# Quantised tiles from row scales in memory in the place of a transpose, in a two-layer kernel on one core

## The chip, the cores and the metric

The kernel runs on one core of a Trainium2 chip. The core has five engines with a queue each: TensorE (PE, matrix products into PSUM), VectorE (DVE), ScalarE (ACT), GpSimd (POOL) and SyncE (SP), which here issues nearly all transfers between memory and SBUF. The metric is the device time of one execution in microseconds. Before the change it is 2084.08 us, the median of three runs (2083.98 to 2085.03).

## What is computed

Two layers over x of 2 x 4096 tokens with 512 channels. In each layer x is normalised, goes through a mixing part and a feed-forward part, and both are added to x. The change touches the feed-forward part of the first layer, a product with x and weights in a 6-bit block format:

```
def _mx_quantize(t, eps=1e-30):
    rows, K = t.shape
    blocks = t.reshape(rows, K // BLOCK_SIZE, BLOCK_SIZE)          # BLOCK_SIZE = 32 channels
    scales = jnp.maximum(jnp.max(jnp.abs(blocks), axis=-1) / FP6_E2M3_MAX, eps)
    q = _nearest_on_grid(blocks / scales[..., None], _GRID)
    return (q, scales)
...
    xq, xs = _mx_quantize(x2)
    wq, ws = _mx_quantize(w2)
    xd = (xq * xs[..., None]).reshape(x2.shape)
    wd = (wq * ws[..., None]).reshape(w2.shape)
    out = xd @ wd.T + bias
...
    x = L0_attn_x
    xn = _layernorm(x, axis=-1)
    x = x + _L0_attn_ref(xn, ...) + _L0_ffn_ref(xn, L0_ffn_weight, L0_ffn_bias)
    xn = _layernorm(x, axis=-1)
    x = x + _L1_attn_ref(xn, ...) + _L1_ffn_ref(xn, ...)
```

`_L0_attn_ref` is two projections, a depthwise convolution, a state-space scan and an output projection; `_L1_attn_ref` is linear attention, whose sums over keys and values are gathered while the first layer's sums are made.

## The kernel before

All work is written out by hand, engine by engine; each engine runs its own list in order, and semaphores join them. Nothing is scheduled by a planner. There are four stages.

**Projection** (`phase_project`, the first 350 us or so). 16 groups of 512 tokens. Per group SP loads x by tokens (for its statistics), x by channels (`x_turned`, 1 MB) and the mean and the root as rows, broadcast over the partitions (`load_rows`). DVE makes the statistics (`statistics`) and normalises x by channels in place (`normalise`, L380, L383); ACT and DVE split it into a high and a low part, since a product in full precision is made of three products; PE projects twice. For the rows, SP stores mean and root to memory (`store_rows`, L244), element by element. The first two groups are normalised by tokens and turned on PE.

**Scan** (`phase_scan`). 64 octets of channels. At its end ACT, DVE, POOL and PE already prepare the first tiles of the next stage.

**Mixing** (`phase_mix`, about 530 to 1300 us). 64 tiles of 128 tokens; the loop variable N of every engine's list stands for the tile whose sums are made. For tile N:
- PE adds two products into the bank of the sums: the scanned part (`scanned`, operand u) and the quantised part (`forward`, operand `qt`). Then it turns the normalised sums of tile N - 1 (`turn_sums`, operand `xn`) and the quantised tile N + 1 (`turn_q`, operand `xq`), both by `turn_in` at L1452, four transposes of 128 x 128. Then `outer` (L1496) of tile N - 3 and `keys` of tile N - 2. It is 48 products of 512 columns and 8 transposes per tile.
- DVE: `low_keys` of N - 3 (L1339); seven steps that quantise tile N + 2 with tokens on the partitions (`prepare_step`, L1311 to L1327: the largest value of each block, scale, inverse, multiply, exponent, rounding number, add it); in even tiles `gate` (L1290), which multiplies u for the next two tiles; `sums` of N (L1348 to L1359), which takes the bank and makes the statistics; `low_n` (L1334); `low_q` of N + 1 (L1296), the low half of the turned quantised tile, out of the bank `BB`; `low_nat` (L1364).
- POOL: `add_keys` of N - 3 (L1113); the root and the shift of the normalisation of tile N (L1117, L1120); in odd tiles `low_u` for the next two (L1105); `finish_quantising` of N + 2: subtract the rounding number (L1084), multiply by the scales (L1086).
- ACT: `keys` (L1197, L1200), `set_keys` (L1189), in odd tiles `high_u` (L1155), `take_turned` (L1206, L1210), `set_sums` (L1179), `high_q` (L1159), `normalise_sums` (L1219, L1224), and `normalise_input` of tile N + 3 (L1167).
- SP: in odd tiles the load of u (y and v, 512 KB each); the store of the sums; the load of x for four tiles on; every second tile a store of the turned sums.

`xq` has three buffers, `qt` two. **Second layer** (`phase_second_layer`): 16 groups; its weights take over buffers of the mixing stage, and its first weights are split on ACT and DVE from tile 50 on.

## Time and profile before

| | us |
|---|---|
| median of three runs | 2084.08 |
| lowest and highest | 2083.98, 2085.03 |
| the profiled execution, its own time | 2084.98 |
| its span | 2083.2 |

| engine | busy us | share |
|---|---|---|
| PE | 2065.6 | 99% |
| DVE | 1521.2 | 73% |
| ACT | 1095.3 | 53% |
| POOL | 839.5 | 40% |

The page gives busy time, the span in 40 slices, the DMA queues, the chain that ended last and the costliest groups of instructions. The engines wait for one another through semaphores, so a busy share doesn't tell how much an engine can be lengthened; the timeline of one stretch does. Two matmuls in a row overlap in the records: a product of 512 columns is recorded with 0.39 us, and the next one starts 0.23 us after it. So on PE starts are to be compared, not durations. TensorE's clock is at its upper level nearly throughout (mean 0.998).

### The profile page before, as it was taken

To read this page: it belongs to the slowest core of one execution; us is meant where nothing else is said; L and a number is where in the kernel's file an instruction comes from. 1 tells how busy PE (TensorE), PEld (TensorE's weight loads), DVE (VectorE), ACT (ScalarE), POOL (GpSimd) and SP (SyncE) were. 2 spreads that over 40 slices of the span, in tenths; PEclk is the share of its full clock that TensorE was granted. 3 is DMA by queue.
4 is the path that set the end of the run, shared out by engine and by line. 5 is a ranking of instruction groups with operands and counts; after the bars stand their busy time and mean duration, and the time that the engine had idled before them with its cause. 6 is when DMAs were issued, how large, how long until landed. Compare 5 with 4: busy or idle time off the path is not lost.

```text
span 2083.2 us, 27336 instructions
## 1 busy us (share of the span) xinstructions
PE 2065.6 (99%) x9263; PEld 1647.1 (79%) x9263; DVE 1521.2 (73%) x2943; ACT 1095.3 (53%) x1842; POOL 839.5 (40%) x842
## 2 busy tenths in 40 slices
PE   9999999999999999999999999999999999999998
PEld 7787888444688888888888888788888888888887
DVE  5898785666687777777777875677777676667776
ACT  4555556323455555555555555754455555555453
POOL 1001110355545444454445453144444444444444
PEclk9999999999999999999999999999999999999999
DMA  5997883886533333333333333422222222222211
GB/s 186 235 222 221 202 219 116 280 255 211 178 115 118 102 118 105 116 118 102 122 107 117 103 128 104 152 71 72 71 71 71 92 91 81 92 71 72 71 41 41
DMA packets 193637, 263.46 MB, mean 126 GB/s; under 512 B 34265, under 2 KB 124633, under 8 KB 190938
## 3 DMA queue, kind: packets, MB, share of 16 engines
q1 hardware_dynamic: 180376, 238.18, 37.7%
q10 hardware_dynamic: 13122, 23.53, 3.0%
q8 instruction: 74, 1.21, 0.2%
q14 instruction: 65, 0.53, 0.1%
HBM read 160.88 MB, written 100.79 MB: 126 GB/s over the span
## 4 chain that ended last, share of the span: by engine, by line
PE 89%; DVE 5%; ACT 2%; issue 2%; POOL 1%; DMA 1%; SPq 0%; POOLq 0%; ACTq 0%
PE bank L102 23%; PE bank L104 23%; PE bank L103 22%; PE bank L1496 7%; PE bank L2052 3%; PE bank L885 3%; PE bank L906 3%; PE bank L903 3%; PE bank L1452 2%; PE bank L629 1%; DVE e_w_lo L1879 0%; DVE d_x L1348 0%; DVE d_xq L1319 0%; DVE d_stats L1350 0%; PE bank L1510 0%
## 5 line engine op out<-in xcount | busy, mean ns | idle before, releaser
L102 PE MATMUL bank<-e_ring,e_w_hi 128*128 128x512 f32 x512 | 200.8, 392 | 0.0
L103 PE MATMUL bank<-e_ring,e_w_hi 128*128 128x512 f32 x512 | 199.3, 389 | 0.0
L104 PE MATMUL bank<-e_ring,e_w_lo 128*128 128x512 f32 x512 | 199.3, 389 | 0.0
L1496 PE MATMUL bank<-d_kh,d_nat 128*128 128x512 f32 x768 | 191.1, 398 | 0.0
L1772 POOL TENSOR_TENSOR e_x<-e_x,e_beta 128x512 f32<-128x512 f32 x64 | 91.3, 1446 | 220.7 <-ACT e_y L1815 220.7
L1117 POOL TENSOR_TENSOR rstd<-d_var_eps,neg_half 128x1 f32<-128x1 f32 x64 | 35.6, 556 | 340.5 <-DVE d_var_eps L1359 340.5
L1826 ACT ACTIVATE e_kr<-bank 128x512 f32<-128x512 f32 x64 | 38.0, 593 | 247.6 <-PE bank L104 247.6
L1496 PEld LDWEIGHTS bank<-d_kh,d_nat 128*128 128x128 f32 x768 | 139.7, 188 | 26.9
L1897 DVE TENSOR_TENSOR e_ring<-e_mixed,e_ring 128x512 fp32r<-128x512 f32 x128 | 93.5, 731 | 88.1 <-ACT e_ring L1790 88.0
L1754 POOL TENSOR_TENSOR e_x<-e_x,e_ff 128x512 f32<-128x512 f32 x64 | 83.3, 1302 | 175.6 <-DVE e_ff L1963 175.6
L1364 DVE TENSOR_TENSOR d_nat<-d_xn,d_nat 128x512 fp32r<-128x512 f32 x64 | 85.9, 1344 | 77.7 <-ACT d_nat L1224 77.7
L1888 DVE SCALAR_TENSOR_TENSOR e_mixed<-e_xt,cols,e_prev 128x512 f32<-128x512 f32 x128 | 104.0, 813 | 41.3 <-ACT e_prev L1801 40.7
L1206 ACT ACTIVATE d_xt<-bank 128x512 f32<-128x512 f32 x64 | 38.2, 597 | 166.9 <-PE bank L1452 166.9
L757 DVE TENSOR_TENSOR_SCAN c_state<-decay,bank 128x255 f32<-128x255 f32 x128 | 80.5, 670 | 52.8 <-PE bank L885 52.6
L308 POOL TENSOR_TENSOR b_rstd<-b_var_eps,neg_half 128x4 f32<-128x4 f32 x16 | 16.2, 1010 | 255.0 <-DVE b_var_eps L364 255.0
L102 PEld LDWEIGHTS bank<-e_ring,e_w_hi 128*128 128x128 f32 x512 | 96.1, 188 | 20.4 <-issue 0.9
L1790 ACT ACTIVATE e_ring<-e_mixed 128x512 fp32r<-128x512 f32 x128 | 80.7, 632 | 59.8 <-DVE e_mixed L1888 57.5
L1758 POOL TENSOR_TENSOR e_y<-e_y,e_att 128x512 f32<-128x512 f32 x64 | 107.0, 1671 | 12.8 <-DVE e_att L1982 12.8
L104 PEld LDWEIGHTS bank<-e_ring,e_w_lo 128*128 128x128 f32 x512 | 96.1, 188 | 20.0
L103 PEld LDWEIGHTS bank<-e_ring,e_w_hi 128*128 128x128 f32 x512 | 96.1, 188 | 19.3
L102 PE MATMUL bank<-e_w_hi,e_keys 128*128 128x512 f32 x256 | 103.7, 405 | 0.1
L102 PE MATMUL bank<-b_xt,b_v 128*128 128x512 f32 x256 | 100.8, 394 | 2.7 <-ACT b_vt L557 2.7
(222 smaller groups left out, 6298.0 us busy)
## 6 DMA issues: line engine op xcount, KB each, us to landing
scr_v<-b_vt SPq DMA_DIRECT2D x64, 256.0 KB, 3.5
scr_z<-b_zt SPq DMA_DIRECT2D x64, 256.0 KB, 5.6
c_z<-scr_z SPq DMA_DIRECT2D x64, 256.0 KB, 4.3
scr_y<-c_y ACTq DMA_DIRECT2D x64, 256.0 KB, 3.9
d_x<-in_L_attn_x SPq DMA_DIRECT2D x64, 256.0 KB, 3.8
d_v<-scr_v SPq DMA_DIRECT2D x32, 512.0 KB, 5.1
scr_x<-d_x SPq DMA_DIRECT2D x64, 256.0 KB, 2.3
scr_xnt<-d_xt SPq DMA_DIRECT2D x32, 512.0 KB, 4.1
```

The costliest lines, as they stand in the source:

```text
L102: eng.matmul(out, lhs[hi], rhs[hi], start=first, stop=False, skip_group_check=onto)
L103: eng.matmul(out, lhs[hi], rhs[lo], start=False, stop=False, skip_group_check=onto)
L104: return eng.matmul(out, lhs[lo], rhs[hi], start=False, stop=last, skip_group_check=onto)
L757: nc.vector.tensor_tensor_scan(state[o % 2][:, b, 1:], rate, SB[o % 2][:, b * NCB:(b + 1) * NCB - 1], 0.0, ALU.mult, ALU.add).then_inc(sta ...
L1364: nc.vector.tensor_tensor(nat[q][:, 1, :], xn[N % 2][:, :], nat[q][:, 0, :].bitcast(F32), ALU.subtract).then_inc(nat_lo, 1)
L1496: mm = pe.matmul(BG[c][:, :], s[:, i, cols], r[:, j, :], start=M % NTB == 0 and i == j, stop=M % NTB == NTB - 1 and i == 1, skip_group_che ...
L1754: nc.gpsimd.tensor_tensor(x2[h][:, t, :], x2[h][:, t, :], ff[t % 2][:, :], ALU.add).then_inc(base_done, 1)
L1758: nc.gpsimd.tensor_tensor(y[t][:, :], y[t][:, :], att[t % 2][:, :], ALU.add).then_inc(sum_done, 1)
L1772: nc.gpsimd.tensor_tensor(x2[h][:, t, :], x2[h][:, t, :], beta[:, :], ALU.add).then_inc(shifted, 1)
L1790: nc.scalar.activation(ring[slot][:, 0, kt, :], src, ACT.Copy).then_inc(hi_done, 1)
L1888: nc.vector.scalar_tensor_tensor(mixed[kt % 2][:, :], current(g % 2, kt), mu[:, kt:kt + 1], prev[kt % 2][:, :], ALU.mult, ALU.add).then_in ...
L1897: nc.vector.tensor_tensor(ring[slot][:, 1, kt, :], src, ring[slot][:, 0, kt, :].bitcast(F32), ALU.subtract).then_inc(lo_done, 1)
```

## The change

From tile 8 on (`BY_ROWS`), x is quantised with channels on the partitions, so that the quantised tile needs no turn before `forward` uses it.

In the mixing stage, for a tile N from 8 to 63:
- SP loads the tile by tokens (`load_tokens`), ACT normalises it (`normalise_tokens`, in the place of `normalise_input`), DVE makes scales and inverses per token and block (`scale_tile`, four steps, the last a transpose of 128 x 32 in blocks of 32 x 32), SP stores them (`store_scales`, 16 KB).
- SP then loads the inverses as a row per block, broadcast over the 32 channels of the block (`load_channels`, 256 KB), and with them the tile by channels out of a new array in which the projection stage has stored normalised x (256 KB); later the scales in the same way (`load_scales`, 256 KB).
- DVE multiplies by the inverse rows, and makes the three rounding steps as before (`row_step`); POOL subtracts, and multiplies by the scale rows. ACT's `high_q` and DVE's `low_q` read the finished tile from SBUF, not from the bank.
- PE leaves `turn_q` out.

In the projection stage SP stores the normalised x of groups 2 to 15 (1 MB each), and the statistics are turned on DVE (`turn_statistics`, two transposes of 128 x 32 per group) and stored in rows of 128 bytes by eight transfers, where two stored single elements. `load_channels` of that stage waits for the low parts alone, behind the store.

What else is in the diff serves room and semaphores: the first buffer `gt` lies where weights of the second layer will be, so their load (at tile 40) and split (at tile 50) wait for PE's use of it; four row buffers lie where the second `gt` will be; several counters are merged into one, with the same waits; the first loads of the scan wait for the stores of normalised x; the second layer's first load waits for `low_q` of the last tile in the place of its turn.

The core of the diff:

```diff
+        def store_normalised(g):
+            if g > TURNED_GROUPS:
+                sp.wait_ge(xn_stored, 16 * (g - TURNED_GROUPS))
+            sp.wait_ge(xn_done, 2 * KT * g)
+            sp.dma_start(scr["xn"][g], xc[g % 2][:, :, :]).then_inc(xn_stored, 16)
...
         def store_rows(g):
-            sp.wait_ge(stat, 4 * g + 4)
-            for w, name in enumerate(("mean0", "rstd0")):
-                sp.dma_start(scr["rows"][g, w].rearrange("a i -> i a"), keep[name][:, g * GT:(g + 1) * GT],
-                             allow_slow_non_contiguous=True).then_inc(rows_out, 16)
+            sp.wait_ge(rows_set, 2 * (g - 1))
+            first = g % (SQUARE // GT) * GT
+            for w in range(2):
+                for s in range(P // SQUARE):
+                    sp.dma_start(scr["rows"][g, w, :, s * SQUARE:(s + 1) * SQUARE],
+                                 turned_stats[w][s * SQUARE + first:s * SQUARE + first + GT, :]).then_inc(rows_out, 16)
...
+        def turn_statistics(g):
+            square = slice(g * GT // SQUARE * SQUARE, (g * GT // SQUARE + 1) * SQUARE)
+            dve.wait_ge(stat, 4 * g + 4)
+            if g > 2:
+                dve.wait_ge(rows_out, 2 * P // SQUARE * 16 * (g - 2))
+            for w, name in enumerate(("mean0", "rstd0")):
+                nc.vector.transpose(turned_stats[w][:, :], keep[name][:, square]).then_inc(rows_set, 1)
...
+    BY_ROWS, ROW_STEPS, SCALE_STEPS = 8, 4, 4
...
+    def load_tokens(N):
+        b, m, h = tile_at(N)
+        if N >= BY_ROWS + 2:
+            sp.wait_ge(s_step, SCALE_STEPS * (N - BY_ROWS - 1))
+        tokens = scr["x"][b].rearrange("(h i m) d -> h i m d", h=2, m=CHUNK)
+        sp.dma_start(xa[N % 2][:, :], tokens[h, :, m, :]).then_inc(xa_ld[N % 2], 16)
+    def store_scales(N):
+        sp.wait_ge(s_step, SCALE_STEPS * (N - BY_ROWS + 1))
+        sp.dma_start(scr["scales"][N].rearrange("c (s i) -> s c i", s=P // QBLOCK), scales_turned).then_inc(s_stored, 16)
+    def row_of(N, w):
+        return bass.AP(scr["scales"].tensor, (N * QBLOCK + w * NBL) * P,
+                       [[KT * P, P // QBLOCK], [0, QBLOCK], [1, KT * P]])
+    def load_channels(N):
+        b, m, h = tile_at(N)
+        sp.wait_ge(s_stored, 16 * (N - BY_ROWS + 1))
+        sp.wait_ge(prep, prep_done(N - 1, 1 if N > BY_ROWS else 0))
+        sp.wait_ge(q_lo, N - 2)
+        sp.dma_start(inv_row[:, :], row_of(N, 0)).then_inc(inv_in, 16)
+        cols = (m % 2 * 2 + h) * P
+        sp.dma_start(xq[N % 3][:, :].rearrange("p (k t) -> p k t", k=KT),
+                     scr["xn"][b * sh.NGB + m // 2][:, :, cols:cols + P]).then_inc(inv_in, 16)
+    def load_scales(N):
+        sp.wait_ge(q_done, N)
+        sp.dma_start(scale_row[:, :], row_of(N, 1)).then_inc(scale_in, 16)
...
         load_part("y", 1, slice(0, KT), u_ld[1])
         for N in range(NT + 1):
+            if BY_ROWS <= N + 3 < NT:
+                load_channels(N + 3)
+            if BY_ROWS <= N + 6 < NT:
+                load_tokens(N + 6)
             if N % 2 and N // 2 + 2 < NT // 2:
                 sp.wait_ge(x2_full, N + 1)
...
             if N + Q < NT:
                 load_x(N + Q)
+            if BY_ROWS <= N + 3 < NT:
+                load_scales(N + 3)
+            if BY_ROWS <= N + 4 < NT:
+                store_scales(N + 4)
             if N and N % 2 == 0:
...
-        pool.wait_ge(prep, PREP * (N + 1))
+        pool.wait_ge(prep, prep_done(N + 1))
         nc.gpsimd.tensor_tensor(tile[:, :], tile[:, :], magic[:, N % 2, :], ALU.subtract).then_inc(q_sub, 1)
         pool.wait_ge(q_sub, N + 1)
+        if N >= BY_ROWS:
+            pool.wait_ge(scale_in, 16 * (N - BY_ROWS + 1))
+            nc.gpsimd.tensor_tensor(tile[:, :], tile[:, :], scale_row[:, :],
+                                    ALU.mult).then_inc(q_done, 1)
+            return
...
+    def quantised(N):
+        return (BB if N < BY_ROWS else xq[N % 3])[:, :].rearrange("p (k t) -> p k t", k=KT)
     def high_q(N):
-        act.wait_ge(q_full, N + 1)
-        nc.scalar.activation(qt[N % 2][:, 0, :, :], BB[:, :].rearrange("p (k t) -> p k t", k=KT), ACT.Copy)\
-          .then_inc(q_hi, 1)
+        if N < BY_ROWS:
+            act.wait_ge(q_full, N + 1)
+        else:
+            act.wait_ge(q_done, N + 1)
+            act.wait_ge(x2_full, N - 1)
+        nc.scalar.activation(qt[N % 2][:, 0, :, :], quantised(N), ACT.Copy).then_inc(q_hi, 1)
+    def normalise_tokens(N):
+        act.wait_ge(xa_ld[N % 2], 16 * ((N - BY_ROWS) // 2 + 1))
+        nc.scalar.activation(xa[N % 2][:, :], xa[N % 2][:, :], ACT.Identity, scale=keep["rstd0"][:, N:N + 1],
+                             bias=shift0[:, N:N + 1]).then_inc(xa_done, 1)
...
-            if N + 3 < NT:
+            if N + 3 < BY_ROWS:
                 normalise_input(N + 3)
+            if BY_ROWS <= N + 5 < NT:
+                normalise_tokens(N + 5)
...
+    def scale_tile(N):
+        n = SCALE_STEPS * (N - BY_ROWS)
+        dve.wait_ge(xa_done, N - BY_ROWS + 1)
+        nc.vector.tensor_reduce(a_max, xa[N % 2][:, :].rearrange("p (b e) -> p b e", e=QBLOCK), AX.X, ALU.max,
+                                apply_absolute_value=True).then_inc(s_step, 1)
+        dve.wait_ge(s_step, n + 1)
+        nc.vector.tensor_scalar(scales[:, NBL:2 * NBL].rearrange("p (s k) -> p k s", k=KT),
+                                a_max.rearrange("p (k s) -> p k s", k=KT), 1.0 / FP6_MAX, SCALE_EPS,
+                                ALU.mult, ALU.max).then_inc(s_step, 1)
+        dve.wait_ge(s_step, n + 2)
+        nc.vector.reciprocal(scales[:, 0:NBL], scales[:, NBL:2 * NBL]).then_inc(s_step, 1)
+        dve.wait_ge(s_step, n + 3)
+        if N > BY_ROWS:
+            dve.wait_ge(s_stored, 16 * (N - BY_ROWS))
+        nc.vector.transpose(scales_turned, scales).then_inc(s_step, 1)
+    def row_step(N, k):
+        tile, p = xq[N % 3], N % 2
+        if k == 0:
+            dve.wait_ge(inv_in, 32 * (N - BY_ROWS + 1))
+            dve.wait_ge(q_done, N - 1)
+            ins_ = nc.vector.tensor_tensor(tile[:, :], tile[:, :], inv_row[:, :],
+                                           ALU.mult)
+        else:
+            dve.wait_ge(prep, prep_done(N, k))
+            ins_ = round_step(tile, magic[:, p, :], k - 1)
+        ins_.then_inc(prep, 1)
...
-            if N + 2 < NT:
+            if N + 2 < BY_ROWS:
                 for k in range(PREP):
                     prepare_step(N + 2, k)
+            elif N + 2 < NT:
+                for k in range(ROW_STEPS):
+                    row_step(N + 2, k)
+            if BY_ROWS <= N + 4 < NT:
+                scale_tile(N + 4)
...
             turn_sums(N - 1)
-            if N + 1 < NT:
+            if N + 1 < BY_ROWS:
                 turn_q(N + 1)
```

On DVE, in an even tile of the mixing stage, before: from `low_keys` over the seven quantising steps and the gate to `sums` (`d_xq` is the quantised tile, `d_ut_raw` is u).

```order
L1339 SCALAR_TENSOR_TENSOR d_kh_106<-bank,d_kh_106 128x512
L1311 TENSOR_REDUCE d_q_max<-d_xq_123 128x16
L1315 TENSOR_SCALAR d_q_scale<-d_q_max 128x16
L1317 RECIPROCAL d_q_inv<-d_q_scale 128x16
L1319 TENSOR_TENSOR d_xq_123<-d_xq_123,d_q_inv 128x512
L1322 TENSOR_SCALAR d_magic<-d_xq_123 128x512
L1325 TENSOR_SCALAR d_magic<-d_magic 128x512
L1327 TENSOR_TENSOR d_xq_123<-d_xq_123,d_magic 128x512
L1290 TENSOR_TENSOR d_ut_raw<-d_ut_raw,d_v_128 128x1024
L1348 TENSOR_TENSOR d_x_109<-bank,d_x_129 128x512
```

The same place after:

```order
L1475 SCALAR_TENSOR_TENSOR d_kh_108<-bank,d_kh_108 128x512
L1429 TENSOR_TENSOR d_xq_130<-d_xq_130,d_inv_row 128x512
L1438 TENSOR_SCALAR d_magic<-d_xq_130 128x512
L1441 TENSOR_SCALAR d_magic<-d_magic 128x512
L1442 TENSOR_TENSOR d_xq_130<-d_xq_130,d_magic 128x512
L1410 TENSOR_REDUCE d_scales<-d_xa_121 128x16
L1413 TENSOR_SCALAR d_scales<-d_scales 128x4x4
L1417 RECIPROCAL d_scales<-d_scales 128x16
L1421 STREAM_TRANSPOSE d_scales<-d_scales 128x32
L1393 TENSOR_TENSOR d_ut_raw<-d_ut_raw,d_v_135 128x1024
L1484 TENSOR_TENSOR d_x_111<-bank,d_x_136 128x512
```

The 512-column steps now stand first, the reduction and the small steps, for another tile, behind them, and the transpose is new.

On SP, in an odd tile of the mixing stage and the even one behind it, before: u, the sums' store, x, and the store of the turned sums.

```order
L1039 DMA d_ut_raw<-scr_y 128x4x256
L1039 DMA d_v_128<-scr_v 128x4x256
L1067 DMA scr_x<-d_x_112 128x512
L1033 DMA d_x_132<-in_L_attn_x 128x512
L1067 DMA scr_x<-d_x_109 128x512
```

After, an odd tile:

```order
L1091 DMA d_inv_row<-scr_scales 128x1x512
L1093 DMA d_xq_129<-scr_xn 128x4x128
L1074 DMA d_xa_122<-in_L_attn_x 128x512
L1112 DMA d_ut_raw<-scr_y 128x4x256
L1112 DMA d_v_134<-scr_v 128x4x256
L1144 DMA scr_x<-d_x_112 128x512
L1106 DMA d_x_137<-in_L_attn_x 128x512
L1098 DMA d_scale_row<-scr_scales 128x1x512
L1078 DMA scr_scales<-d_scales 4x32x32
```

Three loads stand ahead of u now, and the store of the scales is the last of a tile, behind the load of the scale row.

## Rows read from the trace of the kernel before

**Rows 1.** The page, part 1: busy us, share of the span, instructions.
```profile
PE 2065.6 (99%) x9263; PEld 1647.1 (79%) x9263; DVE 1521.2 (73%) x2943; ACT 1095.3 (53%) x1842; POOL 839.5 (40%) x842
```

**Rows 2.** Waits of PE: who waited for whom, us in total, times, longest.
```profile
PE bank L102 <- ACT b_vt L557: 2.7, 1, 2.7
...
PE bank L102 <- POOL d_ut L1105: 2.0, 3, 0.8
```

**Rows 3.** Timeline of PE: start us, us, instruction; two tiles at their turns.
```profile
905.00 0.60 PE L1452 MATMUL bank<-consts,d_xn 128*128 128x128 f32 x4
...
905.79 3.01 PE L1496 MATMUL bank<-d_kh,d_nat 128*128 128x512 f32 x12
...
1291.51 0.60 PE L1452 MATMUL bank<-consts,d_xn 128*128 128x128 f32 x4
1291.87 3.00 PE L1496 MATMUL bank<-d_kh,d_nat 128*128 128x512 f32 x12
```

**Rows 4.** Timeline of DVE over a pair of tiles.
```profile
905.20 0.69 DVE L1348 TENSOR_TENSOR d_x<-bank,d_x 128x512 f32<-128x512 f32 x1 [0.17 <-PE bank L104]
...
917.06 1.22 DVE L1290 TENSOR_TENSOR d_ut_raw<-d_ut_raw,d_v 128x1024 f32<-128x1024 f32 x1
918.19 0.69 DVE L1348 TENSOR_TENSOR d_x<-bank,d_x 128x512 f32<-128x512 f32 x1
...
920.53 0.68 DVE L1296 TENSOR_TENSOR d_qt<-bank,d_qt 128x512 fp32r<-128x512 f32 x1
...
924.45 0.69 DVE L1339 SCALAR_TENSOR_TENSOR d_kh<-bank,d_kh 128x512 fp32r<-128x512 f32 x1 [0.51 <-ACT d_kh L1200]
925.05 0.68 DVE L1311 TENSOR_REDUCE d_q_max<-d_xq 128x16 f32<-128x512 f32 x1
...
926.26 0.69 DVE L1319 TENSOR_TENSOR d_xq<-d_xq,d_q_inv 128x512 f32<-128x512 f32 x1
...
927.91 0.69 DVE L1327 TENSOR_TENSOR d_xq<-d_xq,d_magic 128x512 f32<-128x512 f32 x1
928.78 0.69 DVE L1348 TENSOR_TENSOR d_x<-bank,d_x 128x512 f32<-128x512 f32 x1 [0.17 <-PE bank L104]
```

**Rows 5.** Timeline of ACT, the first of its five activations in the even tile.
```profile
921.05 0.82 ACT L1219 ACTIVATE d_xn<-d_x,shift,rstd 128x512 f32<-128x512 f32 x1 [1.02 <-POOL shift L1120]
```

**Rows 6.** Timeline of POOL: `low_u` of the odd tile, the shift of the even one.
```profile
907.98 2.41 POOL L1105 TENSOR_TENSOR d_ut<-d_ut_raw,d_ut 128x1024 fp32r<-128x1024 f32 x1
...
920.75 0.27 POOL L1120 TENSOR_SCALAR shift<-rstd,d_moments 128x1 f32<-128x1 f32 x1
```

**Rows 7.** Groups of DVE by line and form, 560 to 1290 us: busy us, mean ns.
```profile
L1364 DVE TENSOR_TENSOR d_nat<-d_xn,d_nat 128x512 fp32r<-128x512 f32 x63 | 85.3, 1355 | 75.8 <-ACT d_nat L1224 75.8
...
L1296 DVE TENSOR_TENSOR d_qt<-bank,d_qt 128x512 fp32r<-128x512 f32 x61 | 41.8, 685 | 3.3
```

**Rows 8.** Timeline of DVE at two places where POOL is busy as well.
```profile
571.04 2.38 DVE L1364 TENSOR_TENSOR d_nat<-d_xn,d_nat 128x512 fp32r<-128x512 f32 x2
...
631.34 1.44 DVE L1319 TENSOR_TENSOR d_xq<-d_xq,d_q_inv 128x512 f32<-128x512 f32 x1
```

**Rows 9.** Timeline of POOL at the same two places.
```profile
571.21 1.67 POOL L1084 TENSOR_TENSOR d_xq<-d_xq,d_magic 128x512 f32<-128x512 f32 x1 [1.14 <-DVE d_xq L1327]
...
630.95 1.29 POOL L1113 TENSOR_TENSOR d_kacc<-d_kacc,d_kr 128x512 f32<-128x512 f32 x1
```

**Rows 10.** DMA issues at 918.9, 919.3 and 906.8: KB each, us to landing.
```profile
scr_x<-d_x SPq DMA_DIRECT2D x1, 256.0 KB, 2.0
d_x<-in_L_attn_x SPq DMA_DIRECT2D x1, 256.0 KB, 3.1
...
d_x<-in_L_attn_x SPq DMA_DIRECT2D x1, 256.0 KB, 5.2
```

**Rows 11.** Transfers of the statistics' rows: time from issue to landing.
```profile
DMA to landing us min/median/max: 5.1/10.5/16.7
```

**Rows 12.** Stretch of 0.5 us in a 1 MB load: last columns clock, DMA share, GB/s.
```profile
931.00:931.50 0.50, 0.50 (x3) 0.40 (x3) 0.37 (x2) 0.31 (x1) 0.40 (x2) 1.00 1.02 348
```

More of the change, by code:

```diff
@@ L136, in phase_project @@
     rows = sb("b_rows", [P, 2, GN])
+    turned_stats = [sb(f"b_turned{w}", [P, SQUARE]) for w in range(2)]
     const_in, tab_in = sem("b_const_in"), keep["tables_in"]
@@ L276, in sync @@
         for g in range(NG):
+            if TURNED_GROUPS <= g + 1 < NG:
+                store_normalised(g + 1)
             if 2 < g + 2 < NG:
@@ L481, in vector @@
         nc.vector.memset(vt[0][:, 0, :], 0.0).then_inc(warm, 1)
+        for name in ("mean0", "rstd0"):
+            nc.vector.memset(keep[name][:, :], 0.0)
         statistics(0)
@@ L936, in phase_mix @@
     xt = [front(f"d_xt{i}", [P, KT, 2 * P]) for i in range(2)]
-    gt = front("d_gt", [P, KT, D])
+    gt = [nc.alloc_sbuf_tensor_at("d_gt0", [P, KT, D], F32, offset=areas["tables"].begin["e_w_hi0"]),
+          front("d_gt", [P, KT, D])]
+    at = areas["tables"].begin["d_gt"]
+    xa = [nc.alloc_sbuf_tensor_at(f"d_xa{i}", [P, D], F32, offset=at + 4 * D * i) for i in range(2)]
+    inv_row = nc.alloc_sbuf_tensor_at("d_inv_row", [P, D], F32, offset=at + 4 * D * 2)
+    scale_row = nc.alloc_sbuf_tensor_at("d_scale_row", [P, D], F32, offset=at + 4 * D * 3)
     u_pair = [areas["second_weight"].split_tile(f"d_ut{i}", [P, KT, 2 * P]) for i in range(2)]
@@ L957, in phase_mix @@
     ones = rest("d_ones", [P, 1])
-    const_in, sums_set, bias_done = keep["rows_in"], sem("d_sums_set"), sem("d_bias_done")
+    scale_area = rest("d_scales", [P, D])
+    scales, scales_turned, a_max = scale_area[:, 0:QBLOCK], scale_area[:, P:P + QBLOCK], scale_area[:, 2 * P:2 * P + NBL]
+    const_in, sums_set = keep["rows_in"], sem("d_sums_set")
     x_ld = keep["x_ld"]
@@ L1648, in phase_second_layer @@
     gamma = over("d_bk", "e_gamma", [P, D])
-    beta = areas["rest"].tile("e_beta", [P, D])
+    beta = over("d_scales", "e_beta", [P, D])
     den = small("e_den", [P, 2, 2, HP])
```

115 lines of the change are left out of this document (65 added, 50 removed).

## Prediction

> **What bounds the kernel now.** I read the views in this order. The busy line of the page: TensorE (PE) is busy for 99% of the span, VectorE (DVE) for 73%, GpSimd (POOL) for 40% [rows 1]. Who PE waited for: 2.7 us once for ScalarE (ACT) in the projection stage, 2.0 us in three waits for the low half of u at the head of the mixing stage, and little else [rows 2]. So PE sets the pace, and what it issues is what the kernel costs. Then the timeline of one pair of tiles in the mixing stage, on PE, DVE, ACT and POOL [rows 3 to 6]: a pair takes 23.58 us (905.20 to 928.78). The pair is the unit because u is loaded, gated and split once for two tiles: `gate` on DVE in even tiles, `low_u` on POOL in odd ones.
>
> The second thing to read is how far the other engines are ahead of PE. DVE, POOL, ACT and DVE again form a chain that closes on itself: `sums` on DVE, the root and the shift on POOL, five activations on ACT, `low_keys` on DVE, the quantising steps, `sums` again. In the even tile the shift ends 2.83 us after `sums` started (918.19; 920.75 and 0.27), the five activations take until `low_keys` starts at 6.26 (924.45), 3.43 us [rows 4 to 6]. With 0.60 for `low_keys` and 3.47 for the steps the chain needs 10.3 us in the even tile and 11.5 in the odd one, which has the gate (1.13) after its steps: 21.8 a pair. So PE leads by 1.8 us and no more, which the busy share of 73% doesn't show.
>
> **What the change takes off PE.** 56 of the 64 tiles lose the four transposes of their quantised tile. Both turns take 0.79 us (905.00 to 905.79); the one tile that has only the turn of the sums takes 0.36 (1291.51 to 1291.87) [rows 3]. That is 0.43 us a tile, 56 x 0.43 = 24.1 us, and the pair on PE falls to 22.7 us. It is the gain if nothing else is late.
>
> **What it does to the chain.** The terms:
> - DVE's steps stand in another order. The four row steps of 512 columns come first (0.73, 0.46, 0.46, 0.61 from start to start; 926.26 to 927.91 holds the first three) [rows 4], then, for a tile two further on, the reduction (0.72), two small steps (0.20, 0.29) and a new 32-column transpose. No such transpose is in the trace; its bounds are a small instruction, 0.06, and one of 512 columns, 0.69; I take 0.20, as the other small ones. ACT has as many instructions as before.
> - `low_q` reads two operands in SBUF instead of one there and one in PSUM. The subtraction of that form (L1364), which meets a POOL instruction nearly always, has a mean of 1355 ns; the same one with an operand in PSUM (L1296), beside POOL as well, has 685 [rows 7]. In full: the multiplication that starts at 631.34 ends at 632.78, 0.54 after POOL's `add_keys` (630.95, 1.29) ended; and of two subtractions in a row from 571.04 on, 2.38 together, the second let POOL's go first, which had waited since 571.21 [rows 8, 9]. So the two engines take turns, one instruction each; a POOL instruction of 1.29 that had to wait ends 1.15 after DVE's.
> - The Trainium skill has this as a rule that speaks against the change ("SBUF — State Buffer", "Who interferes with whom"): DVE and GpSimd share a pair of ports as an exclusive lock for the whole instruction, which a DVE instruction with two SBUF inputs needs and a reduction never does. With the lock a pair of tiles comes to 24.95 us here, without it to 22.2, and PE would stay the bound.
>
> With these turns, counted from the start of `sums`. Even tile: root until 2.46, `low_q` (asks at 2.34) until 3.02, shift 3.15 (0.3 later than now), ACT's five 6.58, `low_keys` 7.19; meanwhile POOL's subtraction, multiplication and `add_keys` end at 4.39, 5.75 and 7.44; row steps 7.98, 8.44, 8.90, 9.55; with reduction, small steps and transpose **10.96**. Odd tile: the same until 3.15, then `low_u` 5.51, DVE's `low_nat` 6.05, POOL's subtraction 7.20, `low_keys` 7.19, first row step 7.88, POOL's multiplication 9.03, second row step 9.33, `add_keys` 10.48, the other two 10.80 and 11.45, transpose 12.86, gate **13.99**. Together 24.95 us, over the 23.58 of now.
>
> **The new wait.** `scale_tile` may turn its scales only when the store of the tile before has landed, and SP issues that store behind the load of the scale row, which waits for POOL's multiplication. Odd tile: POOL is done at 9.03, SP issues the load and at 9.6 the store; with a landing of L the gate ends at 9.6 + L + 0.20 + 1.13 = 10.93 + L, later than 13.99 from L = 3.06 on. Even tile: 6.35 + L + 0.20, later than 10.96 from L = 4.4 on. Behind the transpose are queued the gate, `sums`, `low_q` and `low_nat`; PE and POOL's next root wait for them. The bounds of L: 2.0 us for a 256 KB store in a quiet queue, 3.1 for a transfer right behind another, 5.2 behind a megabyte [rows 10]; the statistics' stores, of 4-byte pieces, land in 5.1 at the least [rows 11]. This store has 128 pieces of 128 bytes, behind 256 KB; I take 4.2, the middle of 3.1 and 5.2. Odd tile 15.13, pair 26.09: 2.51 more than now, times 28 pairs = **+70.3 us**. PE's 24.1 us are in this, as gaps.
>
> **The rest.** Projection: two DVE transposes more per group (0.4 us); eight stores of 128-byte pieces in the place of two of 4-byte ones on SP; and the normalised x is stored, 14 MB more ahead of SP's loads. DVE is late once so far, where PE waits 2.7 us [rows 2], and would be by two such pairs more: +1.0 us; bounds 0 and 20 (1.4 us in each of 14 groups, should loads come late). Scan: its first loads and POOL's tables also wait for the stores of x, issued ahead of the last group: 0. Mixing stage, SP's queue: the channels of a tile are issued when its scales have landed, 8 us ahead of their row step, against 5.2 for a slow transfer; the load of u stands behind the tokens' load, which waits for DVE's scales, up to 1 us, with 12 us to the gate: 0. ACT's `high_q` waits for POOL instead of PE, a tile earlier: 0. Moved buffers and merged semaphores: 0.
>
> Sum against the profiled execution: 2084.98 (2083.2 of span and 1.8 around it) + 70.3 + 1.0 = 2156.3; it lay 0.9 over the median, so **2155 us**.
>
> **Rivals.**
> 1. *Not slower: PE stays the bound.* Without any turn lost the chain is 10.5 + 11.7 = 22.2 us a pair. If it keeps under 22.7, the 24.1 us are gained: 2084.1 - 24.1 + 1 = 2061. It decides at the row steps of the odd tile, which must find POOL idle, and at L, which must be under 2.5 (POOL is then done at 7.8). For it: nothing makes PE wait today, and POOL's phase against DVE may shift. Against: the odd tile has 7 us of POOL work behind `sums`, and the means of rows 7 show how often the two meet. 14%.
> 2. *In between.* Only `low_q` and one row step lose a turn and L is small: 22.2 + 0.85 = 23.05 a pair, -15 us: 2070. 8%.
> 3. *The rows go through few queues.* The source of the row loads begins with an extent of 4. Should such a transfer use 4 of the 16 engines, then 256 KB, 0.75 us of all 16 at the 348 GB/s of a full stretch [rows 12], take 3.0, the load lands at 5.3 and the store behind it has L = 5.3: 16.2 + 11.85 = 28.1 a pair, +127: 2211. No transfer of that form is in the trace of before, for or against. The Trainium skill, "DMA: Bandwidth & Descriptors", "Why a DMA increments its semaphore by 16 and not by 1", has it as a rule: a transfer uses as many engines as divide both outermost extents. 22%.
> 4. *The projection becomes bound by its transfers*, on top of the forecast: 2175. 6%.
>
> **How the numbers follow.** The forecast has 50%; its own range is 2123 (L up to 3.06, pair 24.95) to 2205 (L = 5.2, pair 27.9). The transpose at its bounds moves it by -8 and +27 us. To hold 8 in 10 the range takes in rivals 2, 3 and 4: 2070 to 2220; outside are rival 1 and a tail above. A measurement can tell about 0.2% (4 us) from no change. Faster: 0.14 and most of rival 2, 0.20; within: 0.03; slower: 0.77.
>
> **What the profile of after would show.** 32 transposes of quantised tiles left on PE, of 256. The forecast is right where PE has gaps of 1 to 5 us a pair, ended by POOL's low half of u or by DVE's `low_keys`; where `low_q` and the first row steps have means near 1 us; and where the new transpose waits for the store of the scales once a pair. That store's landing against 3.06 and 5.3 tells the forecast's halves and rival 3 apart. It is wrong if PE has no gaps in the mixing stage and a pair takes 22.7 us, or if the gaps lie in the first 360 us.

## The result and the profile after

The changed kernel takes **2201.86 us** (median of four runs, 2201.17 to 2205.36); the kernel before, run beside it, 2084.03. The ratio is 1.0573 (95% interval 1.056 to 1.0585): 118 us slower, where 71 were forecast. The profiled execution has a span of 2199.4 us, 116.2 more than before.

First the busy line of the page, the chain that ended last (shares of the span), and the waits (who waited for whom: us in total, times, longest) of the kernel after.

```profile
PE 2090.2 (95%) x9039; PEld 1649.9 (75%) x9039; DVE 1582.2 (72%) x3029; ACT 1092.2 (50%) x1842; POOL 890.7 (40%) x842
...
PE 61%; DMA 13%; POOL 13%; DVE 8%; issue 2%; ACT 1%; SPq 1%; POOLq 0%; DVEq 0%; ACTq 0%
```

```profile
PE bank L102 <- POOL d_ut L1192: 92.4, 27, 5.2
DVE d_scales L1421 <- DMA scr_scales<-d_scales: 89.4, 51, 2.9
```

PE, which waited 2.0 us for the low half of u before [rows 2], now waits 92.4. It issues 224 transposes fewer (9263 - 9039) and is busy for longer, 2090.2 against 2065.6; why is told below. The second wait is new: DVE's transpose of the scales waits in 51 of 56 tiles for the store of the tile before. The chain gives DMAs 13% of the span and, by line, that one transfer 12%, though it moves 16 KB.

Where the time went is read from the sums' starts: the line of the sums in the kernel before and after (instructions; min/median/max ns; first and last start).

```profile
L1348 DVE TENSOR_TENSOR d_x<-bank,d_x x64: 680/686/692, 555.3 to 1291.5; 128x512 f32<-128x512 f32 x64
```

```profile
L1484 DVE TENSOR_TENSOR d_x<-bank,d_x x64: 664/686/692, 550.8 to 1407.7; 128x512 f32<-128x512 f32 x64
```

The first sums start 4.5 us earlier, the last 116.2 later, which is the whole difference of the spans. So the mixing stage costs 120.7 us more (856.9 against 736.2), what lies ahead of it gives 4.5 back, and the second layer is as it was.

One pair of tiles on DVE, after (compare rows 4):

```profile
906.05 0.69 DVE L1484 TENSOR_TENSOR d_x<-bank,d_x 128x512 f32<-128x512 f32 x1
...
910.75 1.31 DVE L1500 TENSOR_TENSOR d_nat<-d_xn,d_nat 128x512 fp32r<-128x512 f32 x1 [1.67 <-ACT d_nat L1323]
...
913.79 1.38 DVE L1438 TENSOR_SCALAR d_magic<-d_xq 128x512 uint32<-128x512 uint32 x1
915.21 1.39 DVE L1441 TENSOR_SCALAR d_magic<-d_magic 128x512 f32<-128x512 f32 x1
...
918.17 0.25 DVE L1417 RECIPROCAL d_scales<-d_scales 128x16 f32<-128x16 f32 x1
920.79 0.21 DVE L1421 STREAM_TRANSPOSE d_scales<-d_scales 128x32 f32<-128x32 f32 x1 [2.37 <-DMA scr_scales<-d_scales]
920.92 1.18 DVE L1393 TENSOR_TENSOR d_ut_raw<-d_ut_raw,d_v 128x1024 f32<-128x1024 f32 x1
922.02 0.69 DVE L1484 TENSOR_TENSOR d_x<-bank,d_x 128x512 f32<-128x512 f32 x1
...
934.05 0.21 DVE L1421 STREAM_TRANSPOSE d_scales<-d_scales 128x32 f32<-128x32 f32 x1 [1.23 <-DMA scr_scales<-d_scales]
934.18 0.69 DVE L1484 TENSOR_TENSOR d_x<-bank,d_x 128x512 f32<-128x512 f32 x1
```

The odd tile takes 15.97 us, the even one 12.16, the pair **28.13** (23.58 before). Two things are to be seen. The masking step, 0.43 us where nothing is in its way, takes 1.38 and 1.39; and the transpose waits 2.37 us in the odd tile and 1.23 in the even one. The queue of SP says why it waits:

```profile
914.92 0.54 SPq L1098 DMA_DIRECT2D d_scale_row<-scr_scales  x1
915.50 0.54 SPq L1078 DMA_DIRECT2D scr_scales<-d_scales  x1
920.71 0.51 SPq L1091 DMA_DIRECT2D d_inv_row<-scr_scales  x1
```

The load of the inverse rows (L1091) waits for the same store and is issued at 920.71: L = 5.2 us (5.5 in the even tile, 928.43 to 933.97). Over the stage, from the store's issue to the start of the transpose that waits, it is 5.5 in the median of 51 tiles. Ahead of the store stands the row load. The stretch from 914 to 922 us in 40 slices of 0.2, busy share of the 16 DMA engines in tenths and GB/s:

```profile
DMA  9999976565331122262222222222100000000000
GB/s 379 420 410 364 435 266 241 220 241 195 149 62 51 51 72 102 92 184 102 102 102 92 113 92 113 82 85 58 38 24 14 6 0 0 0 0 0 0 0 0
```

Up to 915 us the large transfers run at 364 to 435 GB/s. Then, from 916.8 to 919.4 with hardly anything else under way, some 100 GB/s at a share of 0.2 to 0.3, as much as four engines of sixteen make. 2.6 us at that rate are the 256 KB of rows. The small store follows in the last microsecond.

And what PE does behind a wait:

```profile
911.66 0.62 PE L102 MATMUL bank<-d_w,d_ut 128*128 128x512 f32 x1 [2.76 <-POOL d_ut L1192]
912.07 0.63 PE L103 MATMUL bank<-d_w,d_ut 128*128 128x512 f32 x1
```

```profile
911.70:915.00 3.30, 3.30 (x8) 2.59 (x9) 2.90 (x4) 1.29 (x3) 3.22 (x3) 0.52 1.04 361
```

The third number from the end of the second fence is the granted clock: 0.52, the lower of TensorE's two levels (1.2 of 2.4 GHz). After 2.76 us without work eight products start 0.43 us apart in the place of 0.227, and so PE is busy for longer though it does less. It costs PE some 1.6 us at such a gap, but hardly the kernel: DVE's sums wait for PE's bank 5 times in 64, 10.6 us in all. The spread kernel below has hardly any gaps, and its mean clock is 0.999, against 0.975 here.

### The profile page after: what moved, and what is told of

It is laid out like the page before. It is cut to its first block, busy times and chain, and to the rows that moved or that the text cites. A ratio compares the mean times of both kernels' runs of the same rounds, so it can differ in the third digit from the quotient of the medians.

```text
span 2199.4 us, 27479 instructions
## 1 busy us (share of the span) xinstructions
PE 2090.2 (95%) x9039; PEld 1649.9 (75%) x9039; DVE 1582.2 (72%) x3029; ACT 1092.2 (50%) x1842; POOL 890.7 (40%) x842
## 4 chain that ended last, share of the span: by engine, by line
PE 61%; DMA 13%; POOL 13%; DVE 8%; issue 2%; ACT 1%; SPq 1%; POOLq 0%; DVEq 0%; ACTq 0%
PE bank L102 16%; PE bank L103 16%; PE bank L104 16%; DMA scr_scales<-d_scales 12%; POOL d_xq L1166 3%; POOL d_xq L1170 3%; POOL d_ut L1192 3%; PE bank L2193 3%; PE bank L911 3%; PE bank L932 3%; PE bank L929 2%; DVE d_stats L1486 2%; DVE d_x L1484 2%; POOL shift L1207 1%; DVE d_ut_raw L1393 1%
## 5 line engine op out<-in xcount | busy, mean ns | idle before, releaser
L102 PE MATMUL bank<-d_w,d_ut 128*128 128x512 f32 x256 | 120.4, 470 | 96.3 <-POOL d_ut L1192 92.4
L1500 DVE TENSOR_TENSOR d_nat<-d_xn,d_nat 128x512 fp32r<-128x512 f32 x64 | 91.7, 1433 | 101.7 <-ACT d_nat L1323 101.7
L102 PEld LDWEIGHTS bank<-d_w,d_ut 128*128 128x128 f32 x256 | 57.8, 226 | 122.3 <-issue 102.6
L103 PE MATMUL bank<-d_w,d_ut 128*128 128x512 f32 x256 | 115.3, 450 | 0.0
L104 PE MATMUL bank<-d_w,d_ut 128*128 128x512 f32 x256 | 114.8, 449 | 0.0
L102 PEld LDWEIGHTS bank<-e_ring,e_w_hi 128*128 128x128 f32 x512 | 96.1, 188 | 20.3 <-issue 0.9
```

Source lines behind the costliest of these rows:

```text
L102: eng.matmul(out, lhs[hi], rhs[hi], start=first, stop=False, skip_group_check=onto)
L103: eng.matmul(out, lhs[hi], rhs[lo], start=False, stop=False, skip_group_check=onto)
L104: return eng.matmul(out, lhs[lo], rhs[hi], start=False, stop=last, skip_group_check=onto)
L1500: nc.vector.tensor_tensor(nat[q][:, 1, :], xn[N % 2][:, :], nat[q][:, 0, :].bitcast(F32), ALU.subtract).then_inc(nat_lo, 1)
```

## Experiments

Theory A, formed from the forecast and this profile: the chain that closes over DVE, POOL and ACT sets the pace; it is lengthened by turns on the port that DVE and POOL share, and by the wait for the scales' store, whose L is 5.2 because the row load ahead of it runs on 4 engines. Against it: the wait only fills time that is lost anyway (B), L is due to backlog or small pieces, or transfers as such are the bound (C).

### The store ahead of the row load

```diff
-            if BY_ROWS <= N + 3 < NT:
-                load_scales(N + 3)
             if BY_ROWS <= N + 4 < NT:
                 store_scales(N + 4)
+            if BY_ROWS <= N + 3 < NT:
+                load_scales(N + 3)
```

> The changed kernel, but SP issues the store of the scales ahead of the load of the scale row, as soon as the sums are stored and x is loaded, some 4 us earlier. Theory A (the chain through DVE is the bound, and the transpose's wait for the store is part of it): the transpose's waits (89.4 us in 51 tiles) go, a pair of tiles falls from 28.1 to between 24.5 and 25.0 us, 2202 falls to about 2115 (2105 to 2125). Theory B (the turns that DVE and POOL take on their shared ports set the pace, and the wait for the store only fills time that would be lost anyway to POOL or PE): a pair stays over 27 us, 2175 to 2202. If PE alone set the pace once the wait is gone, a pair would take 22.7 us and the kernel 2056.

2122.24 us (ratio 1.019, 1.0173 to 1.0207). 79.6 us of the 118 are gone by exchanging two issues. The sums on DVE:

```profile
909.89 0.68 DVE L1484 TENSOR_TENSOR d_x<-bank,d_x 128x512 f32<-128x512 f32 x1
...
920.83 0.67 DVE L1484 TENSOR_TENSOR d_x<-bank,d_x 128x512 f32<-128x512 f32 x1
...
934.85 0.68 DVE L1484 TENSOR_TENSOR d_x<-bank,d_x 128x512 f32<-128x512 f32 x1
```

10.94 and 14.02 us; over the 16 tiles around them the means are 10.94 and 13.98. The transpose waited in 2 tiles of 56, 1.9 us in all. So B falls: the wait for the store (89.4 us in total) was paid nearly in full. It also shows the rest of the chain without that wait, at 24.92 a pair.

### Each row load in four transfers

```diff
-        sp.dma_start(scale_row[:, :], row_of(N, 1)).then_inc(scale_in, 16)
+        for part, row in row_of(N, 1):          # 32 partitions each, source [[0, 32], [1, 512]]
+            sp.dma_start(scale_row[part, :], row).then_inc(scale_in, 16)
```

and the same for `inv_row`; the store stays behind the load.

> The changed kernel, with each load of a row (inverse or scale) cut in four transfers of 32 partitions each, so that the source's outermost extent is 32 where it was 4; SP issues 6 transfers more per tile, 0.53 us each, and the store of the scales 1.6 us later. Theory A (a transfer whose source begins with an extent of 4 uses 4 of the 16 DMA engines): the rows move at over 200 GB/s in the place of about 100, and the store behind lands 2.5 to 3.5 us after its issue, where it took 5.2 to 5.8; since it is issued later the pair gains only 1 us or so, 28.1 to 27: 2170 (2140 to 2195). Theory B (the landing is long for the backlog of other transfers, or for the store's own 128-byte pieces): it stays at 5 us or more, and the later issue makes the pair 1.5 us longer in both tiles: 2230 to 2290.

2123.92 us (1.0197, 1.0181 to 1.0212), far more than was expected of it. SP's queue:

```profile
917.61 1.72 SPq L1101 DMA_DIRECT2D d_scale_row<-scr_scales  x4
919.37 0.55 SPq L1078 DMA_DIRECT2D scr_scales<-d_scales  x1
...
921.35 0.79 SPq L1093 DMA_DIRECT2D d_inv_row<-scr_scales  x2
```

The four issues take 1.72 us, and still the store is back earlier: issued at 919.37, landed before 921.35, L = 1.98 us against 5.2. The same bytes and the same small store, only the form of the transfer ahead is another. So L is long neither for the store's own 128-byte pieces, which are the same here, nor for the backlog: in the even tile of the changed kernel hardly anything else is under way when the store is issued (52 GB/s from 928 to 930 us), and L is 5.5; in the odd tile, where L is 5.2, nothing runs behind it. What is left is the form of the transfer ahead, and the four engines by the share of a quarter seen above. The comparison of the two L flatters it somewhat, since the longer issuing lets the rows run before the store is issued: from the first issue of the rows to the landing it is 5.79 us there (914.92 to 920.71) and 3.74 here. I had expected L of 2.5 to 3.5 us, and the rows at over 200 GB/s; they ran at some 130, in four pieces issued 0.4 us apart. The wait of the transpose fell from 89.4 us to 10.5.

### The projection's part alone

```diff
-    BY_ROWS, ROW_STEPS, SCALE_STEPS = 8, 4, 4
+    BY_ROWS, ROW_STEPS, SCALE_STEPS = NT, 4, 4
```

> The changed kernel with all 64 tiles of the mixing stage on the old path (the bound between the paths at 64 instead of 8): what is left is the projection stage's part (x normalised is stored, 14 MB; the statistics are turned on DVE and stored in 128-byte rows), the moved buffers and the merged counters. By the prediction's sum +1.0: 2085. By the changed kernel's trace, in which the first sums of the mixing stage start at 550.8 where they started at 555.3: 2079.5.

2080.08 us (0.998, 0.9971 to 0.9989), 4 us **faster** than before. The prediction's +1.0 had the wrong sign. The next run tells which half of the part does it.

```diff
-            sp.wait_ge(rows_set, 2 * (g - 1))
-            ...  eight stores of turned_stats
+            sp.wait_ge(stat, 4 * g + 4)
+            for w, name in enumerate(("mean0", "rstd0")):
+                sp.dma_start(scr["rows"][g, w].rearrange("a i -> i a"), keep[name][:, g * GT:(g + 1) * GT],
+                             allow_slow_non_contiguous=True).then_inc(rows_out, 16)
```

> The kernel with the projection part alone (2080 us), with the statistics stored as single elements again by two transfers per group, and without the two transposes on DVE; the store of normalised x and the order of the loads stay. If the gain of 4 us of the projection part comes from the form of the statistics' store: back to 2084 or above, with PE's gap of 2.7 us near 61 us again. If it comes from the order of loads: 2080.

2084.27 us (1.0001, 0.9992 to 1.001): the gain is gone, with x still being stored. SP's queue with single elements, and PE:

```profile
48.62 0.38 SPq L251 DMA_DIRECT2D scr_rows<-mean  x1
...
59.82 0.33 SPq L259 DMA_DIRECT2D b_rows<-scr_rows  x1
...
60.67 0.91 SPq L230 DMA_DIRECT2D b_xg<-in_L_attn_x  x2
```

```profile
60.44 0.80 PE L102 MATMUL bank<-b_xt,b_v 128*128 128x512 f32 x1 [2.66 <-ACT b_vt L579]
```

and with the changed kernel's eight pieces of 128 bytes per row:

```profile
46.28 2.63 SPq L253 DMA_DIRECT2D scr_rows<-b_turned  x8
...
53.44 0.39 SPq L261 DMA_DIRECT2D b_rows<-scr_rows  x1
...
54.97 1.69 SPq L230 DMA_DIRECT2D b_xg<-in_L_attn_x  x2
```

SP waits at the row load for what it has stored, 11.2 us from the first issue with single elements (48.62 to 59.82), 7.2 with the pieces (46.28 to 53.44); the loads of the next groups stand behind and come 5.7 us later (2.3 us of it are there already when the stores are issued, 48.62 against 46.28). The one gap of PE in the projection [rows 2] comes with it.

### What PE's turn is worth

```diff
-        turn_in(BB, xq[N % 3], q_full)
+        turn_in(BB, xq[N % 3], q_full, KT if N < 8 else 1)
```

> The kernel before, with one of the four transposes of the quantised tile instead of four, from tile 8 on (three quarters of the turned tile are left out, so the output isn't the reference's). Everything else, ScalarE's and VectorE's reads of the bank too, stays. If PE sets the pace as the prediction has it, three quarters of 0.43 us go in 56 tiles: 18 us, 2066 (2064 to 2069), and a pair takes 22.9 us. If the chain through DVE were already the bound and PE only looked busy, the kernel stays at 2084.

2070.52 us (0.9939, 0.9925 to 0.9953). PE:

```profile
909.56 0.60 PE L1452 MATMUL bank<-consts,d_xn 128*128 128x128 f32 x4
910.00 0.27 PE L1452 MATMUL bank<-consts,d_xq 128*128 128x128 f32 x1
910.03 3.01 PE L1496 MATMUL bank<-d_kh,d_nat 128*128 128x512 f32 x12
```

The turns take 0.47 us in the place of 0.79 [rows 3], 0.32 less as reckoned, and a pair 22.99 in the mean in the place of 23.58. Of the 18 us expected 13.6 came. That PE set the pace before is shown for most of the stage. Where the missing 4 us are, the starts of the sums tell: the pairs of tiles 33 and 34 and of tiles 49 to 54 take as long as before (25.04, 23.62, 23.97 and 24.74 us against 25.06, 23.62, 23.96 and 24.75), so there something else sets the pace, and 2.6 us are lost; the other pairs gain 0.58 us in the mean and not 0.64.

### POOL's instruction off the chain, cut short

```diff
-            nc.gpsimd.tensor_tensor(kacc[b][:, :], kacc[b][:, :], kr[M % 2][:, :], ALU.add).then_inc(kacc_done, 1)
+            wide = D if M < BY_ROWS else 32
+            nc.gpsimd.tensor_tensor(kacc[b][:, 0:wide], ..., kr[M % 2][:, 0:wide], ALU.add).then_inc(kacc_done, 1)
```

> The kernel with the store first (2122 us), and POOL's add_keys, from tile 8 on, over 32 columns instead of 512 (the key sums are left out for the rest, so the output isn't the reference's). The instruction is not on the chain that closes over DVE; POOL has slack of 5 us a tile. If DVE and POOL take turns on a shared port: the row steps no longer wait for it; the masking step falls from a mean of 0.9 us to 0.5 and the pair from 24.95 to about 23.6, 2085 (2078 to 2095). If DVE's times don't depend on what POOL does: no change, 2122.

2108.38 us (1.0116, 1.0102 to 1.013). The two masking steps, by line (busy us, mean ns of one), with the full `add_keys` and with the narrow one:

```profile
L1438 DVE TENSOR_SCALAR d_magic<-d_xq 128x512 uint32<-128x512 uint32 x49 | 44.2, 902 | 1.7
L1441 DVE TENSOR_SCALAR d_magic<-d_magic 128x512 f32<-128x512 f32 x50 | 32.0, 640 | 1.7
```

```profile
L1440 DVE TENSOR_SCALAR d_magic<-d_xq 128x512 uint32<-128x512 uint32 x51 | 26.6, 522 | 1.8
L1443 DVE TENSOR_SCALAR d_magic<-d_magic 128x512 f32<-128x512 f32 x51 | 22.8, 446 | 1.8
```

DVE's instructions of one operand and a constant, which have no data in common with `add_keys`, get 0.38 and 0.19 us shorter when that is cut. So the two engines do take turns. The time, though, fell by 14 us and not by 37: in the odd tile the steps were done sooner, and the transpose then waited for the store again, 16.3 us in 19 of the tiles; the first row step, too, waited longer for its channels (11.9 us against 7.4):

```profile
896.68 2.86 SPq L1144 DMA_DIRECT2D scr_x<-d_x  x1
...
900.42 0.56 SPq L1078 DMA_DIRECT2D scr_scales<-d_scales  x1
...
906.83 0.51 SPq L1091 DMA_DIRECT2D d_inv_row<-scr_scales  x1
```

SP itself needed 2.86 us for one issue that otherwise takes 0.5, and the store landed 6.4 us after its own.

### The scales made in DVE's gap

```diff
-            if BY_ROWS <= N + 4 < NT:
-                scale_tile(N + 4)           # ahead of the gate and sums(N)
...
                 low_q(N + 1)
+            if BY_ROWS <= N + 4 < NT:
+                scale_tile(N + 4)           # ahead of low_nat(N)
```

> The changed kernel, but DVE makes the scales (reduction, two small steps, transpose) behind low_q, where it now waits 1.7 us for ScalarE's high half of the natural sums, and not behind the row steps. Theory A (the chain that closes over DVE is the bound, with the store's wait in it): both go off the chain, since the store has 3 us more to land; what is left is 24.5 less 0.7 to 1.35 us per tile, 21.8 to 23.1 a pair, and PE needs 22.7: 2056 if PE sets the pace, up to 2070; if the small steps have to wait for POOL's instructions there, up to 2090. Theory C (the transfers are the bound: the inverse rows or the channels land too late): 2150 or more, with a wait of the first row step for a transfer.

2131.63 us (1.0234, 1.0219 to 1.025), 70 us better than the changed kernel and still far from 2056. The rival has its share: the first row step waits for its transfers (us in total, times, longest), the gate for u (32.9 us in 28 waits), and the small step waits for POOL's `low_u`:

```profile
DVE d_xq L1429 <- DMA d_xq<-scr_xn: 72.3, 48, 3.1
```

```profile
906.81 1.85 DVE L1413 TENSOR_SCALAR d_scales<-d_scales 128x16 f32<-128x16 f32 x1
```

The reduction now stands 2.9 us behind the sums of its tile, where it stood 4.8 us ahead of them in even tiles and 2.6 in odd ones. Moving the maker of a thing later moved its store, its load and the user's wait as well. The gap is only of use if the inputs of what is put there are ready a tile earlier.

### All three together, and the scales spread

The rows in four transfers, the store first, and DVE's work spread: `low_q`, the small steps and the transpose directly behind the sums, `low_n`, then the reduction of the **next** tile; tokens are loaded and normalised one tile earlier.

```diff
-            low_n(N - 1)
             if N + 1 < NT:
                 low_q(N + 1)
+            if BY_ROWS <= N + 4 < NT:
+                scale_tile(N + 4)           # the two small steps and the transpose
+            low_n(N - 1)
+            if BY_ROWS <= N + 5 < NT:
+                reduce_tile(N + 5)
             low_nat(N)
```

> The changed kernel with each row load cut in four, the store of the scales ahead of the load of the scale row, and DVE's making of the scales taken apart and put where DVE waits: behind the sums come low_q, the two small steps and the transpose, low_n, and then the reduction of the next tile, ahead of the wait for ScalarE's high half; tokens are loaded and normalised one tile earlier. Theory A (the DVE-POOL-ACT chain is what the change made too long, 10.95 and 13.98 us without the wait for the store): 1.35 us per tile go off it, 9.6 and 12.7, 22.3 a pair, under PE's 22.7; PE sets the pace again and the 24 us come out: 2056, up to 2070. If the small steps wait for POOL there, as they did up to 1.9 us in the kernel with the scales in the gap: 23.5 to 24 a pair, 2078 to 2092. If the transfers are late: above 2095, with waits of the first row step for its rows.

**2063.89 us** (0.99, 0.9887 to 0.9914): 1% faster than the kernel before. The page, and the pair on PE (busy, then granted clock third from the end):

```profile
PE 2045.0 (99%) x9039; PEld 1619.6 (79%) x9039; DVE 1578.2 (77%) x3029; ACT 1093.3 (53%) x1842; POOL 900.1 (44%) x842
```

```profile
905.30:928.30 23.00, 23.00 (x106) 18.75 (x105) 20.17 (x37) 12.95 (x22) 13.87 (x11) 1.00 0.66 208
```

A pair takes 22.98 us, the first row step no longer waits, and PE has a wait of 0.2 us a pair for the low half of u. Without it PE would need about 22.75 by itself, an estimate from these two numbers. So the change is worth some 20 us, once the chain that it lengthens is shortened elsewhere. Two variants:

```diff
+            low_n(N - 1)
             if N + 1 < NT:
                 low_q(N + 1)
             if BY_ROWS <= N + 4 < NT:
                 scale_tile(N + 4)
-            low_n(N - 1)
```

> The spread kernel (2064 us) with DVE's low_n ahead of low_q again, as in the changed kernel, and the small steps behind low_q. In the spread kernel low_q stands directly behind the sums; in the even tile POOL's root, 0.55 us elsewhere, takes 1.10 beside it, and in the odd tile low_q waits 0.77 us for ScalarE, so that a pair takes 22.98 by DVE's chain and PE waits 0.2 for the low half of u. Theory A (the chain, with the turns on the port, is still the bound by 0.2 us): the pair falls to PE's own 22.75, 28 x 0.23 = 6 us: 2058 (2056 to 2061). If the small steps behind low_q meet POOL's low_u and wait up to 2 us: 2064 to 2085.

2063.21 us (0.9903, 0.9887 to 0.992): no difference to the last, and a miss. The root fell back to 0.55 us and `low_q` waits 0.17, as expected, but the pair is still 22.96. POOL and DVE behind the sums of the odd tile tell why, in the spread kernel and in this one:

```profile
917.84 0.78 POOL L1210 TENSOR_SCALAR shift<-rstd,d_moments 128x1 f32<-128x1 f32 x1
917.88 0.69 DVE L1404 TENSOR_TENSOR d_qt<-d_xq,d_qt 128x512 fp32r<-128x512 f32 x1 [0.77 <-ACT d_qt L1257]
```

```profile
918.55 0.78 POOL L1210 TENSOR_SCALAR shift<-rstd,d_moments 128x1 f32<-128x1 f32 x1
918.59 0.69 DVE L1404 TENSOR_TENSOR d_qt<-d_xq,d_qt 128x512 fp32r<-128x512 f32 x1 [0.17 <-ACT d_qt L1257]
```

The root of 1.10 us was the even tile's; PE waits for `low_u`, which stands behind the odd tile's root, 0.55 us in both kernels, and behind the shift, which runs beside `low_q` in both and takes 0.78 us (0.27 before, rows 6). From the start of these sums to the end of `low_u` it is 5.70 us in both (915.29 to 920.99; 915.99 to 921.69), so the edit left the way on which PE waits as it was. The odd tile takes 13.00 us in both kernels, and that isn't DVE's doing alone: its `low_keys` waits 0.77 us for ScalarE's high half of the keys, which waits 0.35 us for PE's product.

```diff
-        for part, row in row_of(N, 1):
-            sp.dma_start(scale_row[part, :], row).then_inc(scale_in, 16)
+        sp.dma_start(scale_row[:, :], row_of(N, 1)).then_inc(scale_in, 16)
```

> The spread kernel (2064 us) with each row load as one transfer again, with the source's outermost extent of 4. Theory A (such a transfer uses 4 of 16 DMA engines; four of them a pair keep these engines busy 4 x 2.7 us of 23): the rows, and whatever stands behind them in the queue, land late; PE and DVE wait for rows or for u: 2070 to 2110, with waits of the first row step or of the gate for a transfer. If with the store ahead and the scales earlier there is room enough for slow rows: 2064.

2065.72 us (0.9914, 0.9899 to 0.9929), 1.8 more than with four transfers; nearly a miss as well. The slow form costs hardly anything when nobody stands close behind it. Against the kernel with the store first (2122.24), whose rows have the same form, this run also tells what the spreading of DVE's work, with the tokens a tile earlier, is worth: 56.5 us.

```profile
DVE d_xq L1434 <- DMA d_xq<-scr_xn: 6.1, 9, 2.8
```

## Why the prediction was right, and where it wasn't

The direction, the mechanism and the range were right; the size was not. 120.7 us in the mixing stage against 70.3, -4.5 ahead of it against +1.0.

- **PE's gain.** 0.43 us a tile was forecast, and 0.32 measured for three quarters of the turn. 22.7 us a pair was forecast for PE alone, and about 22.75 is what it needs. All of it became gaps in the changed kernel, as the prediction had it.
- **The chain with its turns.** The working gave 10.96 and 13.99 us; without the store's wait the tiles take 10.94 and 13.98. The turns, too, came where the working had them: it let both masking steps of the odd tile wait for POOL (7.88 to 9.33, 9.33 to 10.80), and they take 1.38 and 1.39 us there; with the store first their means over all tiles are 0.90 and 0.64 us for 0.43, and the first row step's is 1.05. One sign was wrong: the profile of after was to show `low_q` with a mean near 1 us, and it stays at 0.68; it gets in while POOL has only its narrow instructions. The transpose takes 0.21 (0.20 taken).
- **The step that failed: L.** The term was "I take 4.2, the middle of 3.1 and 5.2". Measured are 5.2 in the odd tile and 5.5 in the even one. The threshold of the odd tile was 3.06, of the even one 4.4, so each microsecond over 4.4 counts twice a pair, and 4.2 lay just on the side where the even tile costs nothing. The forecast had 26.09 a pair, measured are 28.13.
- **The rival that came true** is the third, with 22%: 4 of 16 engines, L = 5.3, 28.1 a pair, 2211. The time is 9 below that. The stage's 120.7 instead of 127 come from places where the kernel before isn't at 23.58 a pair itself: the pair of tiles 35 and 36, at 29.32 us before, gets only 1.0 us longer, and the 28 pairs get 4.3 longer in the mean, not 4.5. The projection's part takes off another 4.5, and the profiled executions stand 1.6 us closer together than the medians, the other way. The rule of the Trainium skill's page "DMA: Bandwidth & Descriptors" ("Why a DMA increments its semaphore by 16 and not by 1"), by which a transfer spreads over as many engines as divide both outermost extents, agrees with the runs here: 100 GB/s at a share of a quarter for an extent of 4, and a store behind it that lands after 1.98 us where the extent is 32. The mistake was to price a transfer of a form that the trace of before doesn't have by the landing times of other forms, with a rule at hand that said what differs. That 2201.86 lies under the forecast's own upper end of 2205 is luck in part: with the measured 5.2 and 5.5 its sum gives 28.2 a pair and 2214, and the projection's wrong sign and the pair at tile 35 bring it down.
- **The port.** With the narrow `add_keys` the first masking step's mean went from 0.90 to 0.52 us. The Trainium skill's page "SBUF — State Buffer" ("Who interferes with whom") has DVE and GpSimd lock a shared pair of ports for a whole instruction; the run agrees. The prediction's sentence on it names only instructions with two SBUF inputs, while its working lets the masking steps, with one, wait as well; the runs bear the working out. I gave the lock the whole weight of 24.95 against 22.2 a pair, and 24.92 was measured.
- **The projection.** Two transposes and six more stores were weighed as work; what counted was how long SP stands at the row load behind single elements (11.2 us against 7.2), with the loads of the next groups behind it. The cause of PE's one wait was in [rows 2], and the landing times of the elements in [rows 11]; I put it down to DVE. I also read [rows 11] wrongly: its 5.1 us is the shortest landing of the rows' loads, which that view holds as well (5.1 to 7.5 us); the stores of single elements alone land after 7.5 to 16.7 us. The sum didn't use it.
- **What wasn't seen at all**: TensorE's clock behind the gaps. In the mixing stage PE waits for `low_u` 27 times for over 2 us; behind each of the 21 gaps of 2.76 us and more some products start 0.43 us apart; of the six shorter ones (2.05 to 2.54 us) one, of 2.11 us, is followed by such products and five aren't. It explains PE's longer busy time; no run shows that it cost the kernel anything.

## What to carry to other kernels

A small store whose landing an engine waits for should be issued ahead of any large or narrow transfer, and its place in the queue is worth more than its size: exchanging two lines gave 80 us. Look at the outermost extent of both sides of each transfer before pricing it; one of 4 ran at a quarter of the rate here, and it mattered for what stood close behind it (80 us) far more than for itself (1.8 us). When work is taken off the engine that sets the pace, first add up the chain of the others at a tile's length, since what follows is whichever of the two is longer; and where that chain has a gap, fill it with work whose inputs were made a tile earlier.
